# Row work of three groups moved from ScalarE to GpSimd, last outputs in another order, twelve dummy transposes on TensorE

## The chip, the cores and the metric

The kernel runs on one core of one Trainium2 chip. A time is the device time of that core in microseconds (us), from launch to end. A profile of one execution comes beside it: its span runs from the first to the last instruction that the profile shows, and the execution's own time is a little longer than its span.

## The reference

Four blocks run one after the other on `x` of 64 batches of 128 rows of 256 numbers; each adds its result to `x`. Only the last one, and the row normalisation ahead of it, are touched by the change.

```python
x = x + mlstm(layernorm(x), ctx)            # gates, decays, 4 heads
x = x + layernorm(x) @ ternary(weight).T    # 256 x 256
x = x + attention(layernorm(x), ctx)        # softmax over 128 keys
# the feed-forward part:
n = layernorm(x)                            # by row
scale = 127.0 / max(abs(n), axis=-1)        # by row
q = round(n * scale) / scale
gate, up = silu(q @ w_gate.T), q @ w_up.T   # 256 -> 1024, ternary weights
h = gate * up                               # rounded by row in the same way
x = x + quantised(h) @ w_down.T             # 1024 -> 256
```

## The kernel before

Batches are handled in 16 groups of four (`GB = 4`, `NG = 16`). In the first part, up to about 440 us, a turn of a loop works on several groups in different stages. Then a hand-written piece finishes groups 14 and 15 (`fore` and `aft` are their places in the eight PSUM banks), and from 471 us on a loop over 64 blocks, one for each batch, does the feed-forward part. Every engine has its own program, written out by hand in its order; engines meet at semaphores alone.

**The piece in which the dummy transposes stand.** TensorE turns `x1` (stage `T1`), multiplies it with the 256 by 256 weight (`F0`), turns `x2` (`T2`), and makes scores (`SC`), for group 14 and then for group 15. `T1` of group 15 waits for VectorE's `x1_ready`.

**The block loop.** In block i TensorE does `gate_up(i)` (eight matmuls of 512 columns, L704), `product_rows(i-2)` (transposes, L713) and `down(i-4)` (eight matmuls of 256 columns, L723). ScalarE does `silu(i)` (L1016), `whole_products(i-2)` (L1022), `product_t(i-2)` (L1030) and `scale_out(i-5)` (L1037). VectorE does `ffn_mul(i)`: the product (L1544), the largest value of each row (L1551) and its reciprocal (L1554). GpSimd does `product_scales(i)` (L1185, L1188), `ffn_round(i)` (L1196), and `ffn_out(i-5)` (L1205), which adds the residual. Half of each rounded product is turned by TensorE, the other half by a DMA: `whole_products` writes it, SyncE's queue issues the DMA transpose (L451, `product_turned(i-2)`), and `down` waits for it, as does `whole_products` two blocks later. The gate and up banks are single: `gate_up(i+1)` waits for `silu(i)` and for the product of block i.

**What else the block loop carries.** The row work of groups 13, 14 and 15 is done in the loop. It has five steps: normalise (`normalise_rows`, L792, 4 instructions a group), largest value (VectorE), scale (`scale_rows`, L782, 4 instructions), make whole (`whole_rows`, L799, one of 1024 columns), store to `rows_q`. On ScalarE a function `last_rows(i)` puts one such instruction at the end of a block. Group 13 is normalised before the loop. The store (L467) and everything else that SyncE does stand in one queue in a fixed order; when i % 4 is 3 this is a transposing load of rows (L427), `product_turned(i-2)` (L451), then `group_out` (L443, L445: store and load of 512 KB each), and in the next block `product_turned(i-1)`.

**The end.** After the loop ScalarE copies the turned products of blocks 62 and 63, then scales the outputs of the last five blocks; TensorE's `down` needs the bank of two outputs ago to be free (`o_clear`), and `scale_out(i)` waits for the residual add of block i-2 (`f_done`), since its own result has two buffers.

Of the kernel before, what the change touches and what calls it, by code (L numbers as in the profile page):

```python
# [5 lines left out]
P = 128  # L6
# [119 lines left out]
def build(nc, x, ctx_in, ig_w, ig_b, fg_w, fg_b, out_w, w0, wq, wkv, w_gate, w_up, w_down, out):  # L126
    rows_q = nc.dram_tensor("rows_q", [B, P, E], BF16, kind="Internal").ap()
    with ExitStack() as ctx:
# [214 lines left out]
        f_last = sem("f_last")  # L343
        f_done = sem("f_done")
# [36 lines left out]
        def _(sp):  # L381
# [81 lines left out]
            for i in range(B):  # L463
                for g, at in ((NG - 3, 18), (NG - 2, 36), (NG - 1, 54)):
                    if i == at:
                        sp.wait_ge(f_q, g + 1)
                        sp.dma_start(grp(rows_q, g), fq[:, :, :]).then_inc(q_out, 16)  # L467
                if i == FB * (NG - 6):
                    sp.wait_ge(x_out, 16 * NG)
                for g in range(NG - 3, NG):  # L470
                    if i == FB * (g - 1):
                        sp.wait_ge(q_out, 16 * (g + 1) + 16)
                ffn_block(i)
# [10 lines left out]
        def _(pe):  # L484
            pe.wait_ge(consts, 1)

# [9 lines left out]
            def turn(bank, n, m, z, y, w, p, r):  # L496
# [23 lines left out]
                for stage in bank.stages:  # L520
# [135 lines left out]
                    if stage in ("T1", "T2"):  # L656
                        src = x1 if stage == "T1" else x2_last if z == NG - 1 else x2
                        for b in range(GB):
                            o = open_(stage, b)
                            if stage == "T1":  # L660
                                pe.wait_ge(x1_ready, z + 1)
                            else:
                                moved("F0", b)
# [98 lines left out]
        def _(act):  # L762
# [41 lines left out]

            def last_rows(i):

                if 13 <= i < 13 + GB:
                    scale_rows(NG - 3, (i - 13,))
                if i == 17:
                    whole_rows(NG - 3)  # L810
                if 19 <= i < 19 + GB:
                    normalise_rows(NG - 2, (i - 19,), x3)
                if 31 <= i < 31 + GB:
                    scale_rows(NG - 2, (i - 31,))
                if i == 35:
                    whole_rows(NG - 2)
                if 37 <= i < 37 + GB:
                    normalise_rows(NG - 1, (i - 37,), x3_last)
                if 49 <= i < 49 + GB:
                    scale_rows(NG - 1, (i - 49,))  # L820
                if i == 53:
                    whole_rows(NG - 1)
# [217 lines left out]
            for i in range(B):  # L1040
# [7 lines left out]
                last_rows(i)  # L1048
            product_t(B - 2)
            product_t(B - 1)  # L1050
            for i in range(B - DEPTH - 1, B):
                scale_out(i)
# [3 lines left out]
        def _(pool):  # L1056
# [117 lines left out]
            def last_rows(i):  # L1174

                if i == 25:
                    pool.wait_ge(f_n, GB * (NG - 1))
                    power(3, NG - 1)
                if i == 27:
                    shifts(3, NG - 1)  # L1180

# [408 lines left out]
```

## Time and profile before

| | |
|---|---|
| time, median of 3 runs | 677.48 us (677.37 to 678.04) |
| the profiled execution's own time | 679.77 us |
| its span | 677.9 us |
| mean granted TensorE clock | 0.99 |
| block loop, start of the first and of the last `silu` | 471.07 and 661.11 us |

The profile has the busy time of each engine, a row of the span in 40 slices, the chain of work that ended last, and for every group of instructions the time in which its engine sat idle before it. A matmul's end is modelled, so rows of pipelined matmuls overlap by a little.

### The profile page before, as it was taken

The numbers are of one execution on the slowest core, as the hardware profiler recorded it, in microseconds if no ns is written. First come the engines' busy times: TensorE is split into PE (matmuls) and PEld (weight loads), VectorE is DVE, ScalarE is ACT, GpSimd is POOL, SyncE is SP. The second block draws the span as 40 slices with busy tenths as digits, with TensorE's granted clock in tenths as the row PEclk, the third lists the DMA queues.
The fourth block names the chain that finished last, engine by engine and source line by source line (L and its number), as shares of the span: only waits on it lengthen the run. The fifth ranks groups of instructions, "written<-read, shape, count | busy, mean of one in ns | idle before, by whom it ended". The sixth has DMA issues, their size and how long they took to land.

```text
span 677.9 us, 14933 instructions
## 1 busy us (share of the span) xinstructions
PE 636.8 (94%) x4689; PEld 475.0 (70%) x4710; DVE 568.9 (84%) x1481; ACT 524.9 (77%) x1302; POOL 394.2 (58%) x636
## 2 busy tenths in 40 slices
PE   5889999999999999999999999989799999999995
PEld 4668788787887878878778787777355555555563
DVE  4787978888898898887988889887899998899892
ACT  4666787887877869688687777766589988988984
POOL 3355464464644746547455474472467787777775
PEclk9999999999999999999999999999899999999997
DMA  8310202122022120221212201024336868766763
GB/s 297 108 57 7 94 1 94 57 70 95 16 95 72 54 95 20 92 83 44 94 40 87 94 17 64 19 60 156 71 71 163 171 156 170 136 164 160 167 133 110
DMA packets 105409, 63.64 MB, mean 94 GB/s; under 512 B 52845, under 2 KB 105070, under 8 KB 105334
## 3 DMA queue, kind: packets, MB, share of 16 engines
q1 hardware_dynamic: 98470, 59.29, 32.5%
q10 hardware_dynamic: 6864, 3.41, 1.7%
q8 instruction: 40, 0.66, 0.4%
q14 instruction: 35, 0.29, 0.2%
HBM read 29.39 MB, written 20.97 MB: 74 GB/s over the span
## 4 chain that ended last, share of the span: by engine, by line
PE 60%; DVE 14%; ACT 13%; DMA 5%; issue 4%; SPq 2%; POOL 1%; POOLq 0%; DVEq 0%; ACTq 0%
PE bank L704 10%; PE bank L621 9%; PE bank L672 8%; PE bank L651 8%; PE bank L723 5%; DMA us<-usq 4%; PE bank L693 4%; ACT ew L865 4%; PE bank L526 3%; PE bank L589 3%; ACT x2T L832 2%; PE bank L580 2%; DVE st L1239 2%; PE bank L665 2%; PE bank L571 2%
## 5 line engine op out<-in xcount | busy, mean ns | idle before, releaser
L704 PE MATMUL bank<-WGU,fqT 128*128 128x512 bf16 x491 | 122.0, 383 | 7.3 <-DVE vg L1544 3.7
L1110 POOL TENSOR_SCALAR_AFFINE_SELECT D<-D 128x512 f32<-128x512 f32 x64 | 38.4, 636 | 127.4 <-ACT D L856 127.4
L1544 DVE SCALAR_TENSOR_TENSOR vg<-bank,fback,D 128x1024 f32<-128x1024 f32 x64 | 82.0, 1281 | 11.8 <-ACT D L1016 5.7
L704 PEld LDWEIGHTS bank<-WGU,fqT 128*128 128x128 bf16 x512 | 46.9, 98 | 61.5 <-DVE vg L1544 24.0
L1016 ACT ACTIVATE D<-bank,fback 128x1024 f32<-128x1024 f32 x64 | 71.7, 1120 | 19.6 <-PE bank L704 19.6
L1551 DVE TENSOR_REDUCE hmax<-vg 128x1 f32<-128x1025 f32 x64 | 78.1, 1221 | 2.2
L1095 POOL TENSOR_TENSOR rs<-ve,minus_half 128x4 f32<-128x4 f32 x64 | 65.3, 1027 | 22.8 <-DVE ve L1245 20.4
L1196 POOL TENSOR_SCALAR wtmp<-vg,hscale 128x1024 f32<-128x1024 f32 x64 | 71.6, 1119 | 5.8
L1239 DVE BATCH_NORM_STATS2 st<-x 128x6 f32<-128x256 f32 x184 | 64.4, 411 | 2.7
L672 PE MATMUL bank<-W0T,x1T 128*128 128x256 f32 x256 | 60.1, 388 | 2.6 <-DVE C L1346 2.6
L651 PEld LDWEIGHTS bank<-vaug,C 128*128 128x128 f32 x512 | 60.7, 192 | 2.1 <-issue 1.3
L621 PE MATMUL bank<-WX,qcT 128*128 128x268 f32 x256 | 62.0, 396 | 0.0
L651 PE MATMUL bank<-vaug,C 128*128 128x65 f32 x512 | 60.7, 272 | 1.1 <-DVE C L1346 0.9
L589 PE MATMUL bank<-qcT,GT 128*128 128x512 f32 x128 | 60.3, 595 | 0.9 <-ACT GT L970 0.9
L1116 POOL TENSOR_TENSOR hh<-us,head_scale 128x256 f32<-128x256 f32 x64 | 43.4, 686 | 24.8 <-ACT usq L848 16.2
L672 PEld LDWEIGHTS bank<-W0T,x1T 128*128 128x128 f32 x256 | 48.1, 193 | 11.5 <-DVE C L1346 5.3
L621 PEld LDWEIGHTS bank<-WX,qcT 128*128 128x128 f32 x256 | 47.4, 190 | 10.9 <-issue 3.0
L1122 POOL TENSOR_TENSOR hr<-hv,minus_half 128x16 f32<-128x16 f32 x16 | 46.5, 2903 | 14.8 <-DVE hv L1373 14.7
L879 ACT ACTIVATE qn<-xg,shift,rs 128x256 f32<-128x256 f32 x64 | 33.2, 594 | 26.8 <-POOL shift L1102 26.8
L1153 POOL TENSOR_TENSOR vaug<-cg,vg 128x256 f32<-128x256 f32 x64 | 38.5, 630 | 8.3 <-ACT vg L907 7.7
L1022 ACT ACTIVATE usq<-wtmp 128x512 f16<-128x512 f32 x62 | 39.0, 629 | 3.5 <-DMA us<-usq 3.2
L1346 DVE TENSOR_TENSOR C<-bank,D 128x512 f32<-128x512 f32 x64 | 39.6, 677 | 2.5 <-POOL D L1110 2.5
(198 smaller groups left out, 1524.1 us busy)
## 6 DMA issues: line engine op xcount, KB each, us to landing
out_dram<-x SPq DMA_DIRECT2D x30, 512.0 KB, 3.3
xg<-in_x_dram SPq DMA_DIRECT2D x16, 512.0 KB, 3.9
cg<-in_ctx_dram SPq DMA_DIRECT2D x16, 512.0 KB, 4.5
xg<-out_dram SPq DMA_DIRECT2D x8, 512.0 KB, 4.7
cg<-out_dram SPq DMA_DIRECT2D x8, 512.0 KB, 5.5
rows_q<-fq ACTq DMA_DIRECT2D x13, 256.0 KB, 2.3
raw<-in_L_ffn_w_gate_dram SPq DMA_DIRECT2D x1, 1024.0 KB, 8.2
nrm<-in_L_ffn_w_up_dram SPq DMA_DIRECT2D x1, 1024.0 KB, 10.2
```

The costliest lines, as they stand in the source:

```text
L589: mm = pe.matmul(o[:, :], GT[:, c, rows_at * P:(rows_at + 1) * P], turned[:, EC + c, :, :].rearrange("p b t -> p (b t)"), start=(c == 0), ...
L621: mm = pe.matmul(o[:, 0:VG], qcT[p][:, EC + c, b, :], WX[:, c, :], start=(c == 0), stop=(c == EC - 1))
L651: mm = pe.matmul(o[:, h * AUG:(h + 1) * AUG], C[:, b, h, :], vaug[q][:, b, h, :], start=True, stop=True)
L672: mm = pe.matmul(o[:, 0:E], x1T[:, b, c * P:(c + 1) * P], W0T[:, c, :], start=(c == 0), stop=(c == EC - 1))
L704: mm = pe.matmul(ps[k + half], fqT[:, i // 2 % 2, c, i % 2 * P:(i % 2 + 1) * P], WGU[:, c, which, half * 512:(half + 1) * 512], start=(c = ...
L1016: act.activation(fsil[:, s % 2, :], gate, ACT.Silu, scale=fback[:, p, s % FB, 0:1]).then_inc(g_clear, 1)
L1095: pool.tensor_tensor(rs[i][:, :], ve[i][:, :], minus_half[:, 0:GB], ALU.pow).then_inc(rstd[i], 1)
L1122: pool.tensor_tensor(hr[:, :], hv[:, :], minus_half[:, :], ALU.pow).then_inc(h_rstd, 1)
L1196: pool.tensor_scalar(fhr[:, i % 2, :], fh[i % 2][:, 0:INNER], hscale[:, i % FB:i % FB + 1], CODE, ALU.mult, ALU.add).then_inc(f_hr, 1)
L1239: dve.bn_stats(st[i][:, b, :], src[:, b, :]).then_inc(stats[i], 1)
L1544: dve.scalar_tensor_tensor(out=fh[i % 2][:, 0:INNER], in0=up, scalar=fback[:, g % 2, s, 1:2], in1=fsil[:, i % 2, :], op0=ALU.mult, op1=ALU ...
L1551: dve.tensor_reduce(hmax[:, s:s + 1], fh[i % 2], AX.X, ALU.max, apply_absolute_value=True).then_inc(f_hm, 1)
```

## The change

Four edits:

1. On ScalarE `last_rows` goes. On GpSimd the same steps stand at the end of a block: one `scale_row` or `normalise_row` of 256 columns in each of 20 blocks, and `whole_half`, twice 512 columns for a group, in six blocks.
2. The stores of these rows stand at blocks 23, 41 and 55 of SyncE's queue instead of 18, 36 and 54.
3. After the loop ScalarE's `scale_out` of blocks 59 and 60 stand before the copies of blocks 62 and 63.
4. TensorE does 12 transposes of the identity matrix into the bank of `T1` before it waits for `x1` of group 15. Nothing reads them.

```diff
@@ SyncE
-                for g, at in ((NG - 3, 18), (NG - 2, 36), (NG - 1, 54)):
+                for g, at in ((NG - 3, 23), (NG - 2, 41), (NG - 1, 55)):
@@ TensorE
+            def keep_awake(o, count):
+                for _ in range(count):
+                    pe.transpose(o[:, 0:P], ident[:, :], ident[:, :])
...
                             o = open_(stage, b)
+                            if stage == "T1" and z == NG - 1 and b == 0:
+                                keep_awake(o, 12)
                             if stage == "T1":
                                 pe.wait_ge(x1_ready, z + 1)
@@ ScalarE
-            def last_rows(i):
-                if 13 <= i < 13 + GB:
-                    scale_rows(NG - 3, (i - 13,))
-                if i == 17:
-                    whole_rows(NG - 3)
-                if 19 <= i < 19 + GB:
-                    normalise_rows(NG - 2, (i - 19,), x3)
...
-                last_rows(i)
+            scale_out(B - 5)
             product_t(B - 2)
+            scale_out(B - 4)
             product_t(B - 1)
-            for i in range(B - DEPTH - 1, B):
-                scale_out(i)
+            scale_out(B - 3)
+            scale_out(B - 2)
+            scale_out(B - 1)
@@ GpSimd, in last_rows(i)
+                for group, at in ((NG - 3, 12), (NG - 2, 30), (NG - 1, 48)):
+                    if at <= i < at + GB:
+                        scale_row(group, i - at)
+                for group, src, at in ((NG - 2, x3, 16), (NG - 1, x3_last, 34)):
+                    if at <= i < at + GB:
+                        normalise_row(group, src, i - at)
+                for group, at in ((NG - 3, 20), (NG - 2, 38), (NG - 1, 52)):
+                    if i in (at, at + 1):
+                        whole_half(group, i - at)
...
+            def scale_row(g, b):
+                pool.wait_ge(f_sc, 2 * g + 2)
+                pool.wait_ge(f_q, g)
+                pool.tensor_scalar(fr[:, b, :], fn[:, b, :], fs127[:, b:b + 1], CODE, ALU.mult, ALU.add).then_inc(f_r, 1)
...
+            def whole_half(g, k):
+                pool.wait_ge(f_r, GB * g + GB)
+                pool.wait_ge(q_out, 16 * g + 16)
+                some = slice(2 * k, 2 * k + 2)
+                a = pool.tensor_scalar(fq[:, some, :], fr[:, some, :], CODE, None, ALU.subtract)
+                a.then_inc(f_half, 1)
+                if k == 1:
+                    pool.wait_ge(f_half, 2 * (g - NG + 3) + 2)
+                    pool.sem_inc(f_q, 1)
```

What this does to the order of instructions is seen at three places. The first is TensorE's program where groups 14 and 15 are finished: `ident,x` rows are transposes of `x1` or `x2`, `W0T,x1T` is `F0`, `keyT,x2T` is `SC`. Before:

```order
L672 MATMUL bank<-W0T,x1T 128x256 x8
L665 MATMUL bank<-ident,x 128x128 x8
L680 MATMUL bank<-keyT,x2T 128x128 x8
L665 MATMUL bank<-ident,x 128x128 x8
L672 MATMUL bank<-W0T,x1T 128x256 x8
```

and now:

```order
L680 MATMUL bank<-W0T,x1T 128x256 x8
L673 MATMUL bank<-ident,x 128x128 x8
L688 MATMUL bank<-keyT,x2T 128x128 x8
L491 MATMUL bank<-ident 128x128 x12
L673 MATMUL bank<-ident,x 128x128 x8
L680 MATMUL bank<-W0T,x1T 128x256 x8
```

The twelve dummy transposes have come in between `SC` of group 14 and `T1` of group 15. The second place is the block loop where group 13 is scaled. ScalarE before had, from one `silu` (L1016) to the next, a row instruction (L782) at the end:

```order
L1016 ACTIVATE D<-bank,fback 128x1024
L1022 ACTIVATE usq<-wtmp 128x512
L1030 ACTIVATE fhT<-bank 128x512
L1037 ACTIVATE nrm<-bank,hback 128x256
L782 ACTIVATE raw<-raw,magic,fs 128x256
```

GpSimd now has it, behind its residual add (L1226, which was L1205):

```order
L1206 TENSOR_SCALAR hscale<-hinv 128x1
L1209 TENSOR_SCALAR hback<-hmax,mean_abs 128x1
L1217 TENSOR_SCALAR wtmp<-vg,hscale 128x1024
L1226 TENSOR_TENSOR x<-nrm,xg 128x256
L1185 TENSOR_SCALAR raw<-raw,fs 128x256
```

The row instruction has left ScalarE's block of four and stands as the fifth of GpSimd's block. The third place is the end of ScalarE's program, after the last `silu`: L1029 and L1030 copy the turned product of a block, L1037 scales an output. Before:

```order
L1016 ACTIVATE D<-bank,fback 128x1024
L1022 ACTIVATE usq<-wtmp 128x512
L1030 ACTIVATE fhT<-bank 128x512
L1037 ACTIVATE nrm<-bank,hback 128x256
L1029 ACTIVATE us<-bank 128x512
L1030 ACTIVATE fhT<-bank 128x512
L1029 ACTIVATE us<-bank 128x512
L1030 ACTIVATE fhT<-bank 128x512
L1037 ACTIVATE nrm<-bank,hback 128x256 x5
```

and now:

```order
L1005 ACTIVATE D<-bank,fback 128x1024
L1011 ACTIVATE usq<-wtmp 128x512
L1019 ACTIVATE fhT<-bank 128x512
L1026 ACTIVATE nrm<-bank,hback 128x256 x2
L1018 ACTIVATE us<-bank 128x512
L1019 ACTIVATE fhT<-bank 128x512
L1026 ACTIVATE nrm<-bank,hback 128x256
L1018 ACTIVATE us<-bank 128x512
L1019 ACTIVATE fhT<-bank 128x512
L1026 ACTIVATE nrm<-bank,hback 128x256 x3
```

One output has moved ahead of the copies of block 62 and one ahead of those of block 63.

## Rows read from the trace of the kernel before

**Rows 1.** The page: busy time of each engine

```profile
PE 636.8 (94%) x4689; PEld 475.0 (70%) x4710; DVE 568.9 (84%) x1481; ACT 524.9 (77%) x1302; POOL 394.2 (58%) x636
```

**Rows 2.** The `silu` line in five stretches: count, durations in ns, first and last start

```profile
L1016 ACT ACTIVATE D<-bank,fback x9: 1112/1114/1138, 533.1 to 556.4; 128x1024 f32<-128x1024 f32 x9
...
L1016 ACT ACTIVATE D<-bank,fback x5: 1113/1118/1150, 566.4 to 577.8; 128x1024 f32<-128x1024 f32 x5
...
L1016 ACT ACTIVATE D<-bank,fback x5: 1111/1114/1150, 577.8 to 591.1; 128x1024 f32<-128x1024 f32 x5
...
L1016 ACT ACTIVATE D<-bank,fback x9: 1110/1114/1179, 614.4 to 638.2; 128x1024 f32<-128x1024 f32 x9
...
L1016 ACT ACTIVATE D<-bank,fback x9: 1113/1113/1117, 638.2 to 661.1; 128x1024 f32<-128x1024 f32 x9
```

**Rows 3.** Timeline, 520 to 530 us: start, us, engine, line, instruction

```profile
523.68 0.62 ACT L782 ACTIVATE raw<-raw,magic,fs 128x256 f32<-128x256 f32 x1
524.17 1.13 ACT L1016 ACTIVATE D<-bank,fback 128x1024 f32<-128x1024 f32 x1
...
524.85 0.39 PE L713 MATMUL bank<-ident_h,wtmp 128*128 128x128 f16 x4
...
524.12 0.73 POOL L1205 TENSOR_TENSOR x<-nrm,cg 128x256 f32<-128x256 f32 x1
525.47 0.21 POOL L1185 TENSOR_SCALAR hscale<-hinv 128x1 f32<-128x1 f32 x1 [0.62 <-DVE hinv L1554]
```

**Rows 4.** Instructions by line, 428 to 660 us: busy us, mean ns, idle before

```profile
L1196 POOL TENSOR_SCALAR wtmp<-vg,hscale 128x1024 f32<-128x1024 f32 x62 | 69.4, 1120 | 5.6
...
L799 ACT ACTIVATE fq<-raw 128x1024 bf16<-128x1024 f32 x4 | 4.4, 1089 | 0.0
```

**Rows 5.** Waits, 485 to 661 us; SyncE's queue, 554 to 560 us; L451's landing

```profile
POOL hscale L1185 <- DVE hinv L1554: 38.3, 56, 2.6
...
ACT usq L1022 <- DMA us<-usq: 3.2, 4, 1.3
...
558.38 1.49 SPq L451 DMA_TRANSPOSE us<-usq  x1
...
DMA to landing us min/median/max: 2.4/2.5/6.5
```

**Rows 6.** Timeline by engine, 662 to 675 us; and one stretch of the windows

```profile
666.84 0.62 PE L713 MATMUL bank<-ident_h,wtmp 128*128 128x128 f16 x8 [1.33 <-POOL wtmp L1196]
669.00 1.04 PE L723 MATMUL bank<-WD,fhT 128*128 128x256 f16 x4 [1.54 <-ACT nrm L1037]
...
664.68 0.60 ACT L1029 ACTIVATE us<-bank 128x512 f16<-128x512 f16 x1 [1.09 <-PE bank L713]
...
674.39 0.47 ACT L1037 ACTIVATE nrm<-bank,hback 128x256 f32<-128x256 f32 x1 [1.23 <-PE bank L723]
...
666.75 0.72 POOL L1205 TENSOR_TENSOR x<-nrm,cg 128x256 f32<-128x256 f32 x1
...
668.00:669.00 1.00, 0.00 (x0) 0.00 (x0) 0.00 (x0) 1.00 (x4) 0.00 (x0) 0.61 0.00 0
```

**Rows 7.** Timeline, TensorE, 440 to 463 us; windows: PE, PEld, DVE, ACT, POOL, clock

```profile
452.40 1.95 PE L680 MATMUL bank<-keyT,x2T 128*128 128x128 f32 x16
456.72 1.94 PE L665 MATMUL bank<-ident,x 128*128 128x128 f32 x8 [2.37 <-DVE x L1392]
458.45 4.39 PE L672 MATMUL bank<-W0T,x1T 128*128 128x256 f32 x16
...
456.00:457.00 1.00, 0.28 (x2) 0.31 (x3) 0.97 (x3) 0.00 (x0) 0.18 (x1) 0.80 0.00 0
...
460.00:461.00 1.00, 1.00 (x6) 0.87 (x6) 0.48 (x1) 1.00 (x6) 0.00 (x0) 1.00 1.10 384
```

**Rows 8.** Timeline, TensorE, 0 to 60 us: the same eight transposes, twice

```profile
9.44 1.97 PE L571 MATMUL bank<-ident,cg 128*128 128x128 f32 x8
...
25.85 1.04 PE L571 MATMUL bank<-ident,cg 128*128 128x128 f32 x8
```

More of the change, by code:

```diff
@@ L343, in build @@
         f_last = sem("f_last")
+        f_half = sem("f_half")
         f_done = sem("f_done")
@@ L803, in store_rows @@
                 act.dma_start(grp(rows_q, g), fq[:, :, :]).then_inc(q_out, 16)
-            def last_rows(i):
-                if 13 <= i < 13 + GB:
-                    scale_rows(NG - 3, (i - 13,))
-                if i == 17:
-                    whole_rows(NG - 3)
-                if 19 <= i < 19 + GB:
-                    normalise_rows(NG - 2, (i - 19,), x3)
[L813 to L822, printed above, removed]
             def filled(bank, stage, i=0):
@@ L1180, in last_rows, with normalise_row @@
                     shifts(3, NG - 1)
+            def scale_row(g, b):
+                pool.wait_ge(f_sc, 2 * g + 2)
+                pool.wait_ge(f_q, g)
+                pool.tensor_scalar(fr[:, b, :], fn[:, b, :], fs127[:, b:b + 1], CODE, ALU.mult, ALU.add).then_inc(f_r, 1)
+            def normalise_row(g, src, b):
+                pool.wait_ge(shift_ready[3], g + 1)
+                pool.wait_ge(f_r, GB * g)
+                pool.tensor_scalar(fn[:, b, :], src[:, b, :], rs[3][:, b:b + 1], shift[3][:, b:b + 1],
+                                   ALU.mult, ALU.add).then_inc(f_n, 1)
+            def whole_half(g, k):
[7 more added lines that the diff above has]
+                    pool.sem_inc(f_q, 1)
             def product_scales(i):
```

## Prediction

> **What bounds the kernel now.** The page comes first: TensorE is busy for 94% of the span, VectorE 84%, ScalarE 77%, GpSimd 58% [rows 1], and the mean clock is 0.99. So the gain, if there is one, is in places where TensorE waits or runs at half clock, not in a long stretch of relief. The change touches three such places, and for each I read a view of that stretch.
>
> In the block loop I read the starts of `silu`, since one belongs to each block. Blocks 55 to 63 carry no row work: 22.9 us over 8 blocks, 2.86 us each. Blocks 31 to 35, of which four carry a ScalarE row instruction, take 11.4 / 4 = 2.85. But blocks 35 to 39 take 13.3 / 4 = 3.33 and blocks 47 to 55 23.8 / 8 = 2.98 [rows 2]. So the 620 ns instruction as such costs nothing: ScalarE has it in its slack, since its row instruction and the next `silu` start 0.49 us apart [rows 3]. What costs is less regular: `whole_rows` with 1089 ns [rows 4], and the DMA transposes of the products. Those land 2.5 us after issue in the median but up to 6.5 us when the 512 KB store and load stand just ahead of them in SyncE's queue; ScalarE waits for them four times, 3.2 us [rows 5]. A block that has a ScalarE row instruction has no slack left to take up such a wait.
>
> At the end TensorE waits 1.54 us for an output to be scaled, and starts `down(61)` at 669.00, while the transposes before it began at 666.84. In between the clock falls to half: it is 0.61 on average in 668 to 669, when the engine does nothing [rows 6]. Before `T1` of group 15 TensorE waits 2.37 us for `x1`, the clock falls within 456 to 457 us and is full again at 460 [rows 7].
>
> **Part 1, dummy transposes.** `SC` ends at 452.40 + 1.95 = 454.35; `x1` comes at 456.7 [rows 7]. One transpose of this shape takes 1.04 / 8 = 0.13 us at full clock [rows 8], so twelve take 1.6 us and end at 455.9, 0.8 us ahead of the work that waits. They cost nothing; the bank that they write is free by then. If `x1` came 0.8 us sooner they would begin to cost. The idle time shrinks from 2.37 us to about 0.8, so I expect the clock to hold. Then `T1` takes 1.04 and not 1.94, and `F0`'s 16 matmuls, of which 460.0 - 458.45 = 1.55 us ran at half clock, lose half of that, 0.8. `F0` follows `T1` through the ScalarE copies, so its start moves by about 0.5 to 0.7. Sum 1.3 to 1.6; the scores of group 14 are handled by ScalarE and VectorE in that time at an unchanged hour and hold up the next transposes by 0.1 to 0.2. I take **-1.4**. Bounds: 0 (clock falls all the same) and -1.7.
>
> A rule speaks against this. What the rows show: at 9.44 eight transposes took 1.97 us, and 16 us later the same eight took 1.04 [rows 8]; the engine came from half to full clock in a stretch that began with transposes, so I let them count. The Trainium skill ("TensorE: Matmul & The Clock Gate", Part 4: PE-mode transpose) says that a transpose does not count as activity for the clock. By that rule part 1 would be worth 0; by the rows, 1.4. It is the second rival below.
>
> **Part 2, row work off ScalarE.** Removed are 12 scale and 8 normalise instructions of about 620 ns [rows 3] and three `whole_rows` of 1089 [rows 4]. By the pace above the 20 short ones cost nothing in themselves. What I credit: blocks 35 to 39, 4 x (3.33 - 2.89) = 1.8 us, where a `whole_rows` and a rows store (which stood right behind `group_out` at block 36) fell together with a late transpose; blocks 47 to 55, 8 x (2.98 - 2.88) = 0.8; and 0.6 for what is left of the same kind in blocks 13 to 31. **-3.2**; bounds 0 (all of it was DMA latency that stays) and -5.
>
> **Part 3, row work onto GpSimd.** GpSimd waits for VectorE's reciprocal in each block, 38.3 / 56 = 0.68 us on average [rows 5], 0.62 in the block of [rows 3]. The new instruction of 256 columns is not in the trace. From below: a quarter of the 1024-column one of the same kind, 1120 / 4 = 280 ns [rows 4]; from above the two-input add of 256 columns, 730 ns [rows 3]. It is nearest to the first, with a start-up share: I take 0.45. `whole_half` with 512 columns: 0.56 from below by the same row, 1.46 from above (two such adds); it has the same share of start-up on top of 0.56, so I take 0.7. So twenty blocks fit in the wait, and six exceed it by 0.1 to 0.2 with their waits. What is queued behind it on GpSimd is the next `ffn_round`, and TensorE waits for that: the round of block 15 has ended when the add starts, at 524.12, and TensorE's transposes of it come at 524.85 [rows 3]. That slack of 0.7 hides the excess. **0**; bounds 0 and +8.3 (first rival).
>
> **Part 4, the stores.** `whole_half` of a group ends in GpSimd's block 21, 39 or 53. GpSimd is two blocks behind `silu` there: the add that ends GpSimd's block 15 runs from 524.12 to 524.85, and the `silu` at 524.17 is that of block 17 [rows 3]. So the second half of a group is done 0.7 + 0.7 = 1.4 us into block 23, 41 or 55, and SyncE's queue waits until then; its next step there, the load of turned rows, waits for the block's own `gate_up`, and goes out at about 0.9. With 0.57 for the store's issue everything behind it is 1.1 us late. At 41 there is room. At 23 and 55 `group_out` stands behind, and behind that a product transpose, which before goes out 2.0 us into its block (558.38 against `silu` at 556.4) [rows 2, 5] and now 3.0. I take 4.5 to 5.5 us to land, between the median and the longest [rows 5]. ScalarE asks for it behind the `silu` two blocks on, at 2 x 2.86 + 1.1 = 6.8 us, TensorE a little later; it lands at 7.5 to 8.5. Each costs 0.5 to 1.5, I take 0.9: **+1.8**. Bounds: 0 (the queue had room) and +3.
>
> **Part 5, the end.** `scale_out(59)` now fits in ScalarE's wait of 1.09 us ahead of 664.68 [rows 6] but for 0.4, since it needs the add of block 57, which the block's rhythm (one add a block, 2.8 us ahead of that at 666.75) puts at 663.9 to 664.7. `scale_out(60)` needs the add of block 58, 666.75 + 0.72 = 667.5 [rows 6], and delays the copy of block 63 by another 0.4, which then ends at 669.0. TensorE starts `down(61)` behind its last transposes at 667.4 instead of 669.00 and `down(62)` right behind. `down(63)` waits for `scale_out(61)`, which stands behind the copy, 669.4. At half clock a `down` takes 1.7 us (three of them fill 669.00 to 674.3), at full clock half of that. With the clock falling where it fell, at 668.2, `down(63)` ends at 671.8 instead of 674.3 (just ahead of the last output's scaling at 674.39): -2.5. With it full to the end: 670.5, -3.8 (`down(63)` behind 669.4). With it falling one stretch sooner, because all that comes before has moved against it: -1.5. I take **-2.3**. The add, the store and its landing behind the last output, 674.39 to the span's end, stay.
>
> **Sum.** -1.4 - 3.2 + 0 + 1.8 - 2.3 = -5.1 against the profiled execution's 679.77 us: 674.7. That execution is 2.3 us above the median of the runs shown; the same difference on 677.48 gives **672.4 us**, 0.8% faster. A change of 0.2% (1.4 us) is about what a measurement of this kernel can tell from none.
>
> **Rivals.**
>
> *GpSimd becomes the bound (the other side).* Its row instructions cost what the two-input add costs, 0.73 and 0.1 for their waits, and the halves twice 0.73: 20 x (0.83 - 0.6) + 6 x (1.56 - 0.6) = 10.4 us beyond its wait; 0.7 is absorbed once per group, 2.1. 677.5 - 5.1 + 8.3 = 680.7. For: no row shows the instruction. Against: the same operation with the same operands runs 1024 columns in 1120 ns. It decides the sign when the 20 short ones take over about 0.85 us or the halves over about 1.4. Chance 0.06.
>
> *The dummies don't hold the clock.* Part 1 is 0: 673.8. Chance 0.2.
>
> *The relief of ScalarE brings nothing*, because TensorE and the DMA latencies set the pace in any case: 677.5 - 1.4 + 1.8 - 2.3 = 675.6; with the dummies failing too, 677.0, no change. Chances 0.13 and 0.05.
>
> *The stores cost nothing and the relief is whole*: 677.5 - 1.4 - 5 - 2.5 = 668.6, or with the clock full to the end 667.3. Chance 0.12.
>
> *The forecast*: all of it about as above, 670 to 675. Chance 0.44.
>
> **How the numbers follow.** Faster by over 0.2% is below 676.1: the forecast, the dummies' failure, the whole relief and most of the third, 0.44 + 0.2 + 0.12 + 0.12 = 0.88. Slower is the first rival, 0.05 of its 0.06. The rest, 0.07, is no change. The range goes from 668.8, which leaves out the half of the best case, to 675.8, which leaves out the no-change cases and the first rival.
>
> **What would show it.** After: `F0` of group 15 starts by 458.0 and takes 3.7 us, the granted clock 1.00 from 456 to 461, the first `silu` at 469.7. GpSimd's instructions of 256 columns 0.4 to 0.5 us, its wait for VectorE smaller in those blocks but not gone. Blocks 31 to 39 at 2.9 each. A wait for the product's DMA, of `down` or of `whole_products`, at blocks 25 to 26 and 57 to 58. `down(61)` less than 0.2 us behind the last transposes. The forecast is wrong if GpSimd's wait for VectorE disappears and VectorE's product begins to wait for GpSimd, if late DMA transposes are as costly as before at other blocks, or if the clock falls sooner at the end.

## The result: 0.6% slower, and the profile after

The changed kernel takes 682.44 us (median of 8 runs, 681.13 to 683.73); beside it on the same chip the kernel before took 678.35 (8 runs, 676.75 to 680.68). The ratio is **1.0061, 95% interval 1.0044 to 1.0077**: 4.1 us slower, where 5.1 us faster was predicted. The profiled execution took 683.73 us, its span is 681.9.

The page of the kernel after: busy time of each engine, and the row of the granted TensorE clock in 40 slices.

```profile
PE 640.0 (94%) x4722; PEld 476.6 (70%) x4722; DVE 569.9 (84%) x1481; ACT 514.5 (75%) x1279; POOL 412.9 (61%) x662
...
PEclk9989999999999999999999999999899999999989
```

ScalarE has lost 10 us and GpSimd gained 19, as the edit meant [rows 1]. To see where the time went I cut the two spans (677.9 and 681.9 us) at four marks that both have. One of the instructions just ahead of the piece with the dummies starts at 439.90 us before and at 442.17 after: 2.3 us lost in code that is the same in both. They are lost between 33 and 57 us: the granted clock is 0.50 from 36 to 38 us in the changed kernel and 1.00 in the kernel before. That is a matter of the execution and not of the change: of the 17 profiles of this case five have this fall of the clock and twelve don't. From there to the first `silu` the changed kernel is 1.5 us shorter. From the last `silu` to the end it takes 13.2 us, not 16.8: 3.6 shorter. In between stands the block loop, 190.04 us before and 196.88 after: **6.8 longer**. So the loop is the place. (The clock falls at the start of the loop in both, 483.9 to 487.3 us, in blocks 3 and 4, so that is no part of the 6.8.) Its `silu` in the same five stretches as [rows 2] (blocks 20 to 28, 31 to 35, 35 to 39, 47 to 55, 55 to 63), kernel after:

```profile
L1005 ACT ACTIVATE D<-bank,fback x9: 1113/1114/1115, 534.3 to 559.7; 128x1024 f32<-128x1024 f32 x9
...
L1005 ACT ACTIVATE D<-bank,fback x5: 1113/1114/1115, 568.5 to 580.9; 128x1024 f32<-128x1024 f32 x5
...
L1005 ACT ACTIVATE D<-bank,fback x5: 1113/1113/1114, 580.9 to 593.7; 128x1024 f32<-128x1024 f32 x5
...
L1005 ACT ACTIVATE D<-bank,fback x9: 1113/1113/1115, 617.2 to 640.3; 128x1024 f32<-128x1024 f32 x9
...
L1005 ACT ACTIVATE D<-bank,fback x9: 1113/1114/1115, 640.3 to 668.7; 128x1024 f32<-128x1024 f32 x9
```

Blocks 47 to 55 went from 23.8 to 23.1 us, 35 to 39 from 13.3 to 12.8 and 28 to 31 from 10.0 to 8.8, but 20 to 28 from 23.3 to 25.4, 31 to 35 from 11.4 to 12.4, and the last stretch, which carries no row work, from 22.9 to 28.4. The waits say who is late. Kernel after, 485 to 660 us, two lines of the view of waits (us in total, times, longest):

```profile
POOL hscale L1206 <- DVE hinv L1575: 18.4, 28, 2.5
...
ACT usq L1011 <- DMA us<-usq: 9.4, 8, 2.6
```

ScalarE waits 9.4 us for DMA transposes of products, where it was 3.2 [rows 5]; 2.6 of it fall in block 58 and 1.2 in block 26, but 2.5 in blocks 18 and 34, which had no such wait before. GpSimd, which had waited for VectorE in 56 blocks, does so in 28: in half of them it has no time to spare any more. Its new instructions (kernel after, by line, 485 to 669 us: busy us, mean ns, idle before):

```profile
L1197 POOL TENSOR_SCALAR fq<-raw 128x512 bf16<-128x512 f32 x6 | 9.0, 1507 | 0.0
L1185 POOL TENSOR_SCALAR raw<-raw,fs 128x256 f32<-128x256 f32 x12 | 5.8, 480 | 0.0
L1190 POOL TENSOR_SCALAR raw<-qn,rs,shift 128x256 f32<-128x256 f32 x4 | 2.2, 551 | 0.0
```

The 256-column ones take 480 and 551 ns (450 expected). The half of the whole step takes **1507 ns**, not 700. What that does to SyncE's queue is seen at the last store, 638 to 660 us of the kernel after (start, us, instruction), and in the landing of the transpose at 648.06:

```profile
643.62 0.37 SPq L468 DMA_DIRECT2D rows_q<-fq  x1
644.11 1.20 SPq L428 DMA_TRANSPOSE fqT<-rows_q  x1
645.50 1.19 SPq L452 DMA_TRANSPOSE us<-usq  x1
646.75 0.57 SPq L444 DMA_DIRECT2D out_dram<-x  x1
647.36 0.51 SPq L446 DMA_DIRECT2D cg<-out_dram  x1
648.06 1.42 SPq L452 DMA_TRANSPOSE us<-usq  x1
...
DMA to landing us min/median/max: 6.0/6.0/6.0
```

`silu` of block 55 is at 640.33 and of block 56 at 643.66. The store waits for the second half until 3.3 us into block 55, and the product transpose behind `group_out` goes out 4.4 us into block 56. It lands at 654.1. There stand the three instructions that matter most (timeline of the kernel after, 648 to 658 us):

```profile
654.10 0.65 PE L731 MATMUL bank<-WD,us 128*128 128x256 f16 x4 [2.16 <-DMA us<-usq]
654.14 0.63 ACT L1011 ACTIVATE usq<-wtmp 128x512 f16<-128x512 f32 x1 [2.57 <-DMA us<-usq]
...
654.55 3.58 PE L712 MATMUL bank<-WGU,fqT 128*128 128x512 bf16 x8
```

and the windows around them (PE, PEld, DVE, ACT, POOL busy, granted clock, DMA share, GB/s):

```profile
652.00:654.00 2.00, 0.00 (x0) 0.00 (x0) 1.97 (x2) 0.00 (x0) 1.91 (x3) 1.00 1.41 87
654.00:655.00 1.00, 0.90 (x6) 0.58 (x7) 0.36 (x2) 0.86 (x2) 0.44 (x3) 0.77 0.37 72
655.00:656.00 1.00, 1.00 (x4) 0.43 (x3) 0.00 (x0) 0.62 (x2) 0.98 (x1) 0.50 0.00 0
```

TensorE does nothing from 652 to 654, and behind that its clock is at the lower of its two levels (0.50, 1.2 GHz): eight `gate_up` matmuls take 3.58 us, 1.89 two blocks earlier. Block 58 takes 6.04 us and block 59 3.69, where 2.83 and 2.88 are usual.

At the piece with the dummies (timeline of TensorE, 450 to 462 us, and one window, kernel after) the reader sees the twelve, a wait of 0.97 instead of 2.37, and a full clock where it was 0.80 [rows 7]:

```profile
454.67 1.95 PE L688 MATMUL bank<-keyT,x2T 128*128 128x128 f32 x16
456.45 1.47 PE L491 MATMUL bank<-ident 128*128 128x128 f32 x12
458.89 1.09 PE L673 MATMUL bank<-ident,x 128*128 128x128 f32 x8 [0.97 <-DVE x L1413]
...
456.00:457.00 1.00, 1.00 (x12) 1.00 (x11) 0.97 (x6) 0.00 (x0) 0.48 (x1) 1.00 0.06 16
```

And the end, TensorE and ScalarE, 668 to 682 us, against [rows 6]: the `down` at 674.90 follows the transposes at once, and the last one waits 0.24.

```profile
674.44 0.62 PE L721 MATMUL bank<-ident_h,wtmp 128*128 128x128 f16 x8 [1.33 <-POOL wtmp L1217]
674.90 0.60 PE L731 MATMUL bank<-WD,fhT 128*128 128x256 f16 x4
...
677.05 0.61 PE L731 MATMUL bank<-WD,fhT 128*128 128x256 f16 x4 [0.24 <-ACT nrm L1026]
...
678.19 0.47 ACT L1026 ACTIVATE nrm<-bank,hback 128x256 f32<-128x256 f32 x1 [0.82 <-PE bank L731]
```

### The profile page after: what moved, and what is told of

Same layout as the page of the kernel before. It is cut to its first block, busy times and chain, and to the rows that moved or that the text cites. A ratio compares the mean times of both kernels' runs of the same rounds, so it can differ in the third digit from the quotient of the medians.

```text
span 681.9 us, 15001 instructions
## 1 busy us (share of the span) xinstructions
PE 640.0 (94%) x4722; PEld 476.6 (70%) x4722; DVE 569.9 (84%) x1481; ACT 514.5 (75%) x1279; POOL 412.9 (61%) x662
## 4 chain that ended last, share of the span: by engine, by line
PE 57%; DVE 16%; ACT 11%; DMA 5%; POOL 5%; issue 3%; SPq 2%; POOLq 0%; DVEq 0%; ACTq 0%
PE bank L627 9%; PE bank L657 8%; PE bank L680 8%; PE bank L712 8%; DMA us<-usq 4%; PE bank L731 4%; PE bank L701 4%; ACT ew L854 4%; PE bank L532 3%; PE bank L595 3%; DVE vg L1565 2%; DVE hmax L1572 2%; ACT x2T L821 2%; PE bank L586 2%; DVE st L1260 2%
## 5 line engine op out<-in xcount | busy, mean ns | idle before, releaser
L712 PE MATMUL bank<-WGU,fqT 128*128 128x512 bf16 x512 | 126.9, 387 | 4.6 <-DVE vg L1565 3.1
L657 PEld LDWEIGHTS bank<-vaug,C 128*128 128x128 f32 x512 | 62.4, 196 | 2.1 <-issue 1.3
L657 PE MATMUL bank<-vaug,C 128*128 128x65 f32 x512 | 62.3, 276 | 1.1 <-DVE C L1367 0.9
L1113 POOL TENSOR_TENSOR hr<-hv,minus_half 128x16 f32<-128x16 f32 x16 | 46.4, 2899 | 14.5 <-DVE hv L1394 14.4
L731 PE MATMUL bank<-WD,us 128*128 128x256 f16 x256 | 38.5, 273 | 6.0 <-DMA us<-usq 5.8
```

The costliest lines, as they stand in the source:

```text
L657: mm = pe.matmul(o[:, h * AUG:(h + 1) * AUG], C[:, b, h, :], vaug[q][:, b, h, :], start=True, stop=True)
L712: mm = pe.matmul(ps[k + half], fqT[:, i // 2 % 2, c, i % 2 * P:(i % 2 + 1) * P], WGU[:, c, which, half * 512:(half + 1) * 512], start=(c = ...
L731: mm = pe.matmul(o[:, 0:E], turned[c // HALF][i % 3][:, c % HALF * P:(c % HALF + 1) * P], WD[:, c, :], start=(c == 0), stop=(c == IC - 1))
```

## Experiments

Every kernel was timed against the kernel before on its own chip; since the chips differ a little, sums below go by the ratios, 0.001 being 0.68 us.

### The parts alone

**Dummies alone**: the kernel before with `keep_awake` and its call.

```diff
+                            if stage == "T1" and z == NG - 1 and b == 0:
+                                keep_awake(o, 12)
```

> The kernel before with the twelve dummy transposes alone. Theory: they hold the clock, worth 1.5 us, ratio about 0.998; first silu of the loop about 1.5 us sooner relative to the transposes of x1 in group 14. Rival: in most executions the clock falls elsewhere and nothing is gained, ratio 1.000.

677.40 us, ratio 1.0012 (0.9992 to 1.0031). In its profile the piece is 1.5 us shorter, as in the kernel after, and the loop takes 190.4 us. In the whole time nothing of it can be seen. The profile has one more use: blocks 35 to 39 take 12.8 us here, 47 to 55 22.8 and 31 to 35 12.6, so these three differences between the kernels before and after come with the dummies alone, without any row work moved.

**End alone**: the kernel before with the new order of `scale_out` and `product_t` behind the loop.

> The kernel before with only the new order of the last outputs. Theory: from the last silu to the span's end 13.2 to 14.3 us instead of 16.8, ratio 0.995. If the clock falls in the end, only 1.5 us: 0.998.

675.62 us, 0.9975 (0.9958 to 0.9991): -1.7 us. In its profile the end takes 13.1 us.

**Row work and stores alone**: the kernel after without dummies and with the old end.

> The kernel before with the row work on GpSimd and the stores at 23, 41 and 55, without dummies and with the old end. Theory: this carries the whole loss, the loop takes 197 us instead of 190, ratio 1.010 to 1.013. Rival: the loop's loss in the changed kernel's one profile was mostly chance in the DMA transposes, ratio below 1.006.

684.44 us, 1.0113 (1.0092 to 1.0135): +7.7 us. All of the loss is here.

**The whole step back on ScalarE**: the kernel after, with `whole_rows` on ScalarE at blocks 17, 35, 53 and the stores at their old blocks; the 20 instructions of 256 columns stay on GpSimd.

```diff
-                for g, at in ((NG - 3, 23), (NG - 2, 41), (NG - 1, 55)):
+                for g, at in ((NG - 3, 18), (NG - 2, 36), (NG - 1, 54)):
@@ ScalarE, end of block i
+                if i == 17:
+                    whole_rows(13)
...
@@ GpSimd
-                    if i in (at, at + 1):
-                        whole_half(group, i - at)
```

> The changed kernel with the whole step (fq from fr) back on ScalarE, one instruction of 1024 columns at blocks 17, 35 and 53, stores at 18, 36 and 54 as before; scale and normalise stay on GpSimd. Theory (the two-byte halves of 1.5 us on GpSimd and the late stores behind them cost about 7 us): 673 to 675 us, ratio 0.992 to 0.995. Rival (with ScalarE relieved the product's DMA transposes are awaited more often, whoever makes rows whole): 678 or more, ratio 1.000 or above.

676.93 us, 0.9983 (0.9967 to 1.0000). The loss is gone, so the short instructions on GpSimd cost nothing that can be measured; but it is no faster than dummies and end together:

**Dummies and end together**, nothing else of the change.

> The kernel before with the dummy transposes and the new end, without the row work. If the parts add up: 675.6 to 676.5 us (dummies nothing, end -1.7). If the dummies' 1.5 us is kept once the end no longer falls to half clock: 674.

676.05 us, 0.9975 (0.9956 to 0.9994). That is the ratio of the end alone.

### Why the half is slow

**Halves in float32**: the half writes its four-byte source in place of the two-byte `fq`. `rows_q` of the last three groups then holds old numbers, so that part of the computation is left out.

```diff
-                a = pool.tensor_scalar(fq[:, some, :], fr[:, some, :], CODE, None, ALU.subtract)
+                a = pool.tensor_scalar(fr[:, some, :], fr[:, some, :], CODE, None, ALU.subtract)
```

> The changed kernel with its half steps writing float32 back in place of fr instead of two-byte numbers into fq; the last three groups' rows_q then hold old numbers. Theory (the two-byte output makes the instruction of 512 columns 1.5 us long): it takes 0.6 to 0.7 us, GpSimd is late by nothing, SyncE's store goes out at 1.4 to 1.6 us into block 55, and the kernel takes 676 to 678 us, ratio 0.997 to 1.001. Rival (the instruction is long for another reason): 1.5 us and 682.

682.42 us, 1.0062 (1.0042 to 1.0083), and the line of this kernel, 485 to 669 us:

```profile
L1197 POOL TENSOR_SCALAR raw<-raw 128x512 f32<-128x512 f32 x6 | 9.1, 1512 | 0.0
```

Unchanged: the two-byte result is not what makes it slow.

**Halves in two operations**: the same subtraction as a multiplication by 1.0 and an addition.

```diff
+                a = pool.tensor_scalar(fq[:, some, :], fr[:, some, :], 1.0, -CODE, ALU.mult, ALU.add)
```

> The changed kernel with its half step written with two operations (times 1, plus the negative code) instead of one (minus the code), same shape and types. Theory (the instruction with a single subtraction is what is slow, 1.5 us for 512 columns): it takes 0.6 to 0.7 us, the store of group 15 goes out 1.3 to 1.6 us into block 55 instead of 3.3, and the kernel takes 677 to 679.5 us, ratio 0.998 to 1.002. Rival (the type, the shape or the place makes it slow): 1.5 us and 682.

678.02 us, 0.9998 (0.9981 to 1.0016): 4.3 us less than the kernel after. The line, and the last store with the transpose and the wait behind it (timelines of SyncE and ScalarE, 636 to 656 us):

```profile
L1197 POOL TENSOR_SCALAR fq<-raw 128x512 bf16<-128x512 f32 x6 | 3.8, 627 | 0.0
...
639.01 0.37 SPq L468 DMA_DIRECT2D rows_q<-fq  x1
...
643.46 1.43 SPq L452 DMA_TRANSPOSE us<-usq  x1
...
649.56 0.63 ACT L1011 ACTIVATE usq<-wtmp 128x512 f16<-128x512 f32 x1 [2.53 <-DMA us<-usq]
```

It is the form with one operation, a subtraction, that was slow: 1507 ns against 627. Whether the number of operations or the subtraction makes it so is not separated, since both changed. Now the store goes out at 1.7 us into its block, near the 1.4 of the prediction. But the wait in block 58 is still 2.53 us in this execution, and that block and the next take 6.08 + 3.60 us. The execution took 679.18 us, one of the slower half of twelve that go from 675.26 to 680.01; so this is what the late store can still cost, and not what it costs each time.

### GpSimd's lateness, or the store's

**Idle halves**: the kernel with the whole step on ScalarE, and on GpSimd six single-operation subtractions of 512 columns, in the blocks of the real halves, into a tile that nothing reads.

```diff
+                if i in (20, 21, 38, 39, 52, 53):
+                    some = slice(2 * (i % 2), 2 * (i % 2) + 2)
+                    pool.tensor_scalar(spare[:, some, :], fr[:, some, :], CODE, None, ALU.subtract)
```

> The kernel with the whole step on ScalarE (d) and, besides, GpSimd's two-byte halves at the same blocks as in the changed kernel, into a tile that nothing reads. So GpSimd is as late as in the changed kernel, and the stores are not. Theory A (half of the loss is the late rounding, half the late stores): 679.5 to 681. Theory B (the late stores carry it): 677. Theory C (the late rounding carries it): 683.

676.66 us, 0.9989 (0.9974 to 1.0003).

**Idle halves and late stores**: as that, with the stores at 23, 41 and 55, each waiting for the idle halves of its group.

```diff
-                for g, at in ((NG - 3, 18), (NG - 2, 36), (NG - 1, 54)):
+                for g, at in ((NG - 3, 23), (NG - 2, 41), (NG - 1, 55)):
                     if i == at:
                         sp.wait_ge(f_q, g + 1)
+                        sp.wait_ge(f_half, 2 * (g - NG + 3) + 2)
```

> The kernel with idle halves (g), with the stores at 23, 41 and 55 in SyncE's queue and waiting there also for the idle halves. Against g only the stores are late. Theory (the late stores in SyncE's queue carry the loss): 681 to 683 us, ratio 1.005 to 1.008. Rival: 677 to 679, and the loss comes from the true dependence of the halves on GpSimd.

682.09 us, 1.0059 (1.0039 to 1.0078): the whole loss is back. The two kernels do the same work on every compute engine; only the stores move. The waits for product transposes, 485 to 660 us, first with idle halves alone, then with late stores:

```profile
ACT usq L1012 <- DMA us<-usq: 3.9, 5, 1.3
```

```profile
ACT usq L1013 <- DMA us<-usq: 6.8, 6, 2.7
```

**One late store, and two**: the last kernel with only the third store late (18, 36, 55), and with only the first two late (23, 41, 54).

> The kernel with the whole step on ScalarE and idle halves on GpSimd, with the last of the three stores alone late: at block 55 behind the idle halves, the first two at 18 and 36. Theory of one collision: the last one carries most, since in the kernel with all three late blocks 52 to 60 took 28.71 us against 24.58 with none late, and blocks 20 to 28 took 25.22 against 24.39. So 680.7 us, 4.1 above the 676.7 of none late. Rival, a price for each store: a third of 5.4 us, so 678.5 us.

> The same with the first two stores late, at blocks 23 and 41 behind their idle halves, and the third at 54 with no wait for the halves. Theory of one collision: 0.8 us for the first and about nothing for the second, 677.5 us. Rival, a price for each store: two thirds of 5.4 us, 680.3 us.

The third alone: 681.39 us, 1.0048 (1.0034 to 1.0062), 4.0 us above idle halves alone. The first two: 679.09 us, 1.0016 (1.0002 to 1.0030), 1.8 above. Equal prices per store are refuted, and so is the expectation that only one counts: the third costs about 4, the first two about 1.8 together; how these share it was not measured. The sum, 5.8, and the 4.7 of all three agree within the intervals.

**Awake in block 58**: the kernel after with twelve dummy transposes ahead of the `down` that waits in block 58, into the unused half of its bank.

```diff
+                if i == 54:
+                    for _ in range(12):
+                        pe.transpose(o[:, E:E + P], ident[:, :], ident[:, :])
                 pe.wait_ge(h_clear, i + 3)
```

> The changed kernel with twelve more dummy transposes, ahead of the output multiplication that TensorE starts in block 58 and that waits for the late product transpose. Theory of the clock: block 58 and the one behind it take 6.04 + 3.69 us, of which 2.57 are the wait and some 1.7 + 0.8 the clock at half behind it (eight matmuls of 512 columns took 3.58 us there and 1.89 a block before). With the idle stretch filled, block 58 takes 4.2 to 4.5 us and the next 2.9, and the kernel 680.0 us, 1.003 of before. Rival, the wait alone: the clock has nothing to do with it, 682.4 us as the changed kernel.

680.28 us, 1.0040 (1.0023 to 1.0058), 1.4 us less than the kernel after by the ratios. The new instructions, the wait, and the window behind (TensorE's timeline and windows of this kernel):

```profile
651.10 1.48 PE L729 MATMUL bank<-ident 128*128 128x128 f32 x12
...
653.93 0.61 PE L734 MATMUL bank<-WD,us 128*128 128x256 f16 x4 [0.92 <-DMA us<-usq]
...
655.00:656.00 1.00, 1.00 (x6) 0.49 (x5) 0.00 (x0) 1.00 (x3) 1.00 (x2) 1.00 0.03 6
```

The clock holds, blocks 58 and 59 take 5.23 + 2.88 us instead of 6.04 + 3.69, 1.6 less. ScalarE waits as long as before (2.64 us). Of the 4.0 us that these two blocks take beyond the usual, then, 1.6 are the clock and 2.4 the late transpose itself. The medians' gain is smaller than the 1.6, and the 95% intervals of the two ratios overlap. Two more things bear on it. Seven of the twelve executions have a mean granted clock of 0.999 or 1.000 and take 679.2 to 680.6 us, while none of the eight of the changed kernel is above 0.997 or below 681.1. And the fall does not come in each execution: of the six profiles with a wait of 2.1 to 2.3 us in block 58 and no transposes in it, four have it, and in the two others (rows and stores alone, one late store) these two blocks take 8.0 and 8.2 us, as with the transposes.

### Where the dummies' gain goes

**Dummies at the program's start**: the kernel before with twelve transposes ahead of TensorE's first wait for the weights.

> The kernel before with twelve dummy transposes at the very start of TensorE's program, where it is idle until 7.5 us, and none ahead of x1. Theory (the added instructions move TensorE's instruction loads by DMA about 1.5 us sooner in the loop, onto the product transposes that stand behind a store and a load): the product transposes issued in blocks 16, 32 and 56 land after 5.5 us or more, those in 28 and 52 sooner, the loop takes 0.5 to 1.5 us longer, no clock is gained, ratio 1.001 to 1.002. Rival (the landing times are chance): blocks 16, 32 and 56 stay at 4.5.

677.58 us, 0.9991 (0.9975 to 1.0006), but what I expected of the slow transposes was wrong: they stayed at the blocks of the kernel before, and all but two of TensorE's instruction loads in the loop stayed at their hours too.

**End alone, with 128 semaphore increments at TensorE's start.**

```diff
+            for _ in range(128):
+                pe.sem_inc(unused, 1)
             pe.wait_ge(consts, 1)
```

> The kernel before with the new end (b) and 128 semaphore increments that nothing waits for at the very start of TensorE's program, in its idle time. Theory (instruction loads collide with the product transposes): TensorE's loads come some 7 us sooner and fall between the stores; the product transposes issued in blocks 28 and 52 land in about 4.5 us, 1 to 2 us less than b, ratio to the kernel before 0.995 to 0.996. Rival (chance): as b, 0.9975.

690.09 us, 1.0178 (1.0155 to 1.0201): the increments took 19.4 us, far more than I had allowed for, so the time tells nothing. The trace does: the loads on queue q8 stand some 8 us earlier against the loop, while those on q14 keep their place, so q8 is the queue of TensorE's instructions. The transposes behind `group_out` of blocks 28 and 52, which took 6.5 and 5.5 us before, land after 4.6 and 4.6; those of blocks 12 and 44 are slow instead (5.5, 5.7), those of 20 and 36 remain so (5.7, 6.0). The page of transfers of the kernel before, 556 to 566 us, has the load beside the slow one of block 28 (packets, MB, share of 16 engines); from 571 to 578 us of the shifted kernel, around its block 28, there is no such line, and its landing is the second fence.

```profile
q8 instruction: 1, 0.02, 0.6%
```

```profile
DMA to landing us min/median/max: 4.6/4.6/4.6
```

In these traces TensorE's instructions come by DMA, 16 KB every 14 to 26 us in the loop. Read over all profiles, 52 of the 54 product transposes behind `group_out` that had such a load start between 0 and 4.1 us behind their issue took 5.2 to 6.5 us; the two others had gone out late. The 114 with no load of either queue beside them took 3.8 to 4.9. Block 20 was slow beside a load on queue q14 (8 KB), and block 36 in part with none in flight (in the kernel before a store of rows stands just ahead of it), so this is not the only cause. With the dummies in the piece ahead of the loop, blocks 16, 32 and, in most kernels, 56 become slow, and 52 no longer is. That is how 1.5 us gained ahead of the loop can be lost inside it: in the profiles, neither of which has the fall of the clock in blocks 3 and 4, the loop takes 190.8 us with dummies and end, 188.8 with the end alone. Blocks 31 to 35, where the slow transpose of block 32 is awaited, take 12.2 to 12.8 us in all twelve profiles with the dummies there and 11.4 to 11.8 in the five without. That such a load makes a transpose slow is a correlation that one shift confirmed and another (at the start) failed to test, so I call it likely and not shown.

### A version that beats both

**Two-operation halves, one block sooner**: the kernel after with the fast halves; scaling and halves of groups 13 and 15 and the normalising of group 14 one block earlier, and the stores at 22, 42 and 54, where no `group_out` stands right behind.

```diff
-                for g, at in ((NG - 3, 23), (NG - 2, 41), (NG - 1, 55)):
+                for g, at in ((NG - 3, 22), (NG - 2, 42), (NG - 1, 54)):
...
-                for group, at in ((NG - 3, 12), (NG - 2, 30), (NG - 1, 48)):
+                for group, at in ((NG - 3, 11), (NG - 2, 30), (NG - 1, 47)):
-                for group, src, at in ((NG - 2, x3, 16), (NG - 1, x3_last, 34)):
+                for group, src, at in ((NG - 2, x3, 15), (NG - 1, x3_last, 34)):
-                for group, at in ((NG - 3, 20), (NG - 2, 38), (NG - 1, 52)):
+                for group, at in ((NG - 3, 19), (NG - 2, 38), (NG - 1, 51)):
```

> The changed kernel with the two-operation halves, the rows of groups 13 and 15 one block sooner on GpSimd, and the stores at 22, 42 and 54, where no store and load of 512 KB stand right behind them. Theory (what is wrong with the change is the late store ahead of group_out, not row work on GpSimd): no wait for a product transpose over 1 us at blocks 26 and 58; 673.5 to 676 us, ratio 0.994 to 0.997. Rival (row work on GpSimd costs in itself): 678 or more.

674.48 us, 0.9950 (0.9932 to 0.9969): 3.4 us faster than the kernel before, the fastest of all. Against dummies and end together (0.9956 to 0.9994) it is 1.7 us, and the two intervals overlap. Its last store, the transpose behind `group_out` and the wait for it (SyncE and ScalarE, 630 to 648 us; `silu` of block 56 is at 637.90):

```profile
633.83 0.37 SPq L468 DMA_DIRECT2D rows_q<-fq  x1
...
639.84 1.43 SPq L452 DMA_TRANSPOSE us<-usq  x1
...
645.84 0.63 ACT L1011 ACTIVATE usq<-wtmp 128x512 f16<-128x512 f32 x1 [1.14 <-DMA us<-usq]
```

The transpose goes out at 1.9 us into its block, as before the change. It still lands late (5.9 us, an instruction load stands beside it), but the wait is 1.14 us and not 2.5, the clock stays full, and the last eight blocks take 23.7 us instead of 28.4.

## Why the prediction was wrong

**Three terms failed: the price of the half in part 3 (0.7 us put, 1.51 measured), which made the stores of part 4 cost 4.7 us and not 1.8, and part 2, the relief of ScalarE (-3.2 put, about +0.6 measured).** The sum said -5.1 and the measurement +4.1, so 9.2 us are to be explained. By the ratios 4.3 of them go when the half alone is made fast (1.0061 to 0.9998): that is what turned no change into a slower kernel. The other 5.0 are why there was no gain even then, and most of them are part 2.

**Part 4, the stores: +1.8 expected, 4.7 to 5.4 measured** (idle halves with and without late stores, by the ratios and by the medians). The queue was said to wait "until 1.4 us into block 23, 41 or 55"; it waits until 3.3 (block 55), and the product transpose behind `group_out`, put at 3.0, goes out at 4.4. The fault lies in part 3's price of the half, below. The other term is "each costs 0.5 to 1.5". In block 58 of the profile with the fast half it was 6.08 + 3.60 - 2.83 - 2.88 = 4.0 us. The landing of 6.0 us was beyond the 4.5 to 5.5 I took, though [rows 5] had 6.5; and I did not ask what TensorE's clock does behind a wait of over 2 us, while [rows 6] and [rows 7] showed it at 0.61 and 0.80 beside waits of 1.54 and 2.37. By medians this term is less sure: the fast halves with late stores are 3.3 us above the version with the stores moved away (0.9998 against 0.9950), 1.8 expected, and that difference is uncertain by 1.7. The sum of the bounds of this part, +3, left the true size outside. The form was right: waits came at blocks 26 and 58, where the prediction had put them. Those at 18 and 34 it had not; 34 has one in the profile of the dummies alone too (1.0 us), 18 a shorter one (0.6), and neither has one in rows and stores alone.

**Part 3: 256 columns right, the half wrong.** 0.45 was taken, 0.48 and 0.55 measured. For the half 0.7 was taken and 1.51 measured, just over the upper bound of 1.46. The row it was scaled from, L1196, is a `tensor_scalar` with two operations, and the half has one; in two operations it takes 0.63, near the estimate. The conclusion drawn from it, that excess of GpSimd hides in slack, held all the same: six idle halves of 1.5 us cost nothing that can be measured (0.9989 against 0.9983). So the first rival is refuted in its mechanism, though it had the right sign and the trigger it named, halves above 1.4 us, was met (by its own sum, with the 2.1 us that are absorbed, the trigger would have been 1.7): GpSimd did not become the bound, it made a DMA queue late. No rival had that path.

**Part 2, relief of ScalarE: -3.2 expected, about +0.6 measured in the changed kernel.** Moving the short instructions alone gave nothing (0.9983 against 0.9975 of dummies and end), and taking `whole_rows` off ScalarE nothing either while the stores are late (1.0061 against 1.0059). The prediction credited 1.8 us to blocks 35 to 39 and 0.8 to 47 to 55. The profile of the kernel after has 0.5 and 0.7 there, but that of the dummies alone, with all row work on ScalarE, has 0.5 and 1.0: they are not relief. At block 38 the wait for the product transpose stays, 1.6 us. With the stores out of the way all of it gives 0.9975 - 0.9950, 1.7 us, not clear of noise. The reading that 620 ns as such fit in the slack was right; the rest was DMA latency for the most part, the bound of 0 that I had named.

**Part 1, dummies: right at its place, worth nothing in the sum.** 1.5 us measured in the piece, 1.4 expected; `F0` takes 3.69 us at the full clock. The second rival is refuted: the clock fell at this place in all five profiles without the twelve transposes and in none of the twelve with them. The Trainium skill ("TensorE: Matmul & The Clock Gate", Part 4: PE-mode transpose) says that transposes don't count as activity for the clock; here the traces say otherwise, the window 456 to 457 has 1.00 with them and 0.80 without. What I missed is that a gain ahead of the loop is kept only if the loop does not depend on when it starts. Its alignment to the instruction loads seems to matter; that is the likely cause and not a shown one.

**Part 5, the end: right in its form.** 3.6 and 3.7 us less than the kernel before in the profiles, near the full-clock case of 3.8; -1.7 in the median of the end alone, where -2.3 was expected. Why the median has less than half, the other profiles suggest: the old end takes 16.8 us in the kernel before, but 15.9, 15.8 and 14.4 in the three others that have it (dummies at the start, rows alone, dummies alone), by where the clock falls; the new end takes 13.0 to 13.3 in all thirteen. So the gain is 1.1 to 3.8 us by the execution, and [rows 6] showed one of the dearest.

By the ratios, from dummies and end (0.9975): short instructions to GpSimd +0.5 us, idle halves +0.4, late stores +4.7, the halves made real and `whole_rows` off ScalarE +0.1; together 5.8, and with the end's -1.7 the 4.1 of the result. The separate parts do not add like that everywhere: rows and stores alone gave +7.7, and adding dummies and end to them -3.5, twice what the two give by themselves, since each shift moves the collisions.

## What to carry to other kernels

A step that moves behind a slower producer delays everything behind its DMA in the queue, and the price is read from the tightest customer of that queue, not from the queue's average; here half of the product transposes behind `group_out` landed 0.1 to 0.8 us ahead of their use in the kernel before, and the others late. When a wait of TensorE grows, add what the clock may cost behind it (1.6 us here, in four of six profiles). Price an instruction from a row of the same form (operations, operands), not of the same name alone, and move a store to a block where nothing urgent stands behind it.

## What the runs showed of the hardware

- GpSimd's `tensor_scalar` with one operation (subtract) on 128x512 took 1507 to 1512 ns, with a two-byte or a four-byte result; with two operations (multiply, add) 627 ns. Twice the columns with two operations took 1119. Whether the count or the kind of operation matters was not tested.
- A DMA transpose of a product took 2.4 to 2.5 us to land in the median, 3.8 to 4.9 behind a store and a load of 512 KB, and 5.2 to 6.5 in 52 of 54 cases when an instruction load of TensorE started within 4.1 us behind its issue as well.
- Behind 2.2 us without work TensorE's granted clock went to 0.50 and the next eight matmuls took 3.58 us instead of 1.89, in four of six profiles with such a wait; twelve transposes in that stretch kept it at 1.00.
- The clock also falls where nothing differs between the kernels: in blocks 3 and 4, behind a wait of 1.7 us, in 13 of 17 profiles, which makes blocks 0 to 13 41.3 to 41.7 us long instead of 40.3 (42.8 in the two where the fall lasts 6.8 us). A stage that has such a fall in one profile and not in the other says nothing of a change.
- 128 semaphore increments on TensorE's queue took 19.4 us, 0.15 each.
